# Pair attention on one core: the products of two steps made by one VectorE instruction for each half of the fields

## The reference

```
p = x[:, ROW, :]
q = x[:, COL, :]
inner = p * q
h = jax.nn.relu(jnp.einsum('bpe,he->bph', inner, W1) + b1)
logits = jnp.einsum('bph,oh->bpo', h, W2) + b2
attn = jax.nn.softmax(logits, axis=1)
pooled = jnp.sum(inner * attn, axis=1)
return pooled @ Wl.T + bl
```

## Time and profile before

| what | us |
|---|---|
| median of three runs | 1154.47 (1153.91 to 1154.53) |
| the profiled execution | 1153.29 |
| its span in the trace | 1151.4 |
| PE busy (matmuls) | 1128.6 (98%) |
| DVE busy | 1056.9 (92%) |
| ACT busy | 982.9 (85%) |

### The profile page before, as it was taken

The page is one execution under the profiler, slowest core; times in us unless marked ns, Lnnn a source line. Parts: engine busy times, 40 slices in busy tenths (PEclk is TensorE's granted clock), DMA queues, the critical chain, the costliest instruction groups (busy, mean ns, idle before and its releaser), DMA issues.

```text
span 1151.4 us, 63299 instructions
## 1 busy us (share of the span) xinstructions
PE 1128.6 (98%) x29001; PEld 534.3 (46%) x29001; DVE 1056.9 (92%) x1691; ACT 982.9 (85%) x1219; POOL 0.7 (0%) x6
## 2 busy tenths in 40 slices
PE   6999999999999999999999999999999999999995
PEld 3444444444444444444444444444444444444442
DVE  7999999899999989999899998999999999998983
ACT  5888888888888888888888888888888888888884
POOL 0000000000000000000000000000000000000000
PEclk9999999999999999999999999999999999999997
DMA  2221221222121121211312212121122213113010
GB/s 58 42 66 32 61 39 29 62 40 55 36 60 35 37 64 29 66 29 34 69 28 63 40 26 66 35 59 37 30 63 39 57 34 68 30 35 69 14 43 2
DMA packets 220376, 51.31 MB, mean 45 GB/s; under 512 B 216016, under 2 KB 216016, under 8 KB 220112
## 3 DMA queue, kind: packets, MB, share of 16 engines
q1 hardware_dynamic: 220112, 47.27, 20.0%
HBM read 34.11 MB, written 13.12 MB: 41 GB/s over the span
## 4 chain that ended last, share of the span: by engine, by line
PE 98%; DVE 1%; SPq 1%; ACT 0%; DMA 0%; issue 0%; ACTq 0%
PE slot L296 60%; PE logit_bank L316 29%; PE slot L277 4%; PE slot L264 4%; DMA x_rows<-in_r_x 0%; PE slot L342 0%; SPq L193 0%; ACT hidden L369 0%; DVE weighted L468 0%; SPq L223 0%; SPq L227 0%; SPq L225 0%; SPq L230 0%; DVE logits L448 0%; DVE row_max L452 0%
## 5 line engine op out<-in xcount | busy, mean ns | idle before, releaser
L369 ACT ACTIVATE hidden<-slot,b_col 128x780 f32<-128x780 f32 x1024 | 875.9, 909 | 115.9 <-PE slot L296 115.8
L431 DVE TENSOR_TENSOR inner<-xt 128x760 f32<-128x760 f32 x1024 | 909.5, 943 | 58.8 <-PE slot L296 58.1
L296 PE MATMUL slot<-inner,w_block 64*32 64x390 f32 x16384 | 782.8, 490 | 0.0
L296 PEld LDWEIGHTS slot<-inner,w_block 64*32 64x32 f32 x16384 | 300.7, 107 | 326.4 <-issue 281.5
L316 PE MATMUL logit_bank<-hidden,w_window 64*32 64x390 f32 x8192 | 442.1, 487 | 0.6 <-ACT hidden L369 0.6
L316 PEld LDWEIGHTS logit_bank<-hidden,w_window 64*32 64x32 f32 x8192 | 152.8, 105 | 186.4 <-ACT hidden L369 81.5
L277 PEld LDWEIGHTS slot<-xt,x_scaled 64*40 64x40 f32 x4096 | 45.4, 117 | 40.6 <-issue 40.6
L353 ACT COPY xt<-slot 128x640 f32<-128x640 f32 x64 | 44.4, 694 | 19.6 <-PE slot L264 19.6
L361 ACT COPY gram_rows<-slot 128x640 f32<-128x640 f32 x64 | 44.4, 694 | 18.3 <-PE slot L277 18.3
L438 DVE TENSOR_TENSOR inner<-xt 128x80 f32<-128x80 f32 x256 | 59.5, 233 | 0.0
L264 PE MATMUL slot<-ident,x_rows 128*128 128x128 f32 x320 | 50.1, 288 | 9.3 <-DMA x_rows<-in_r_x 9.3
(11 more groups left out here) (28 smaller groups left out, 27.2 us busy)
## 6 DMA issues: line engine op xcount, KB each, us to landing
x_rows<-in_r_x SPq DMA_DIRECT2D x128, 160.0 KB, 3.0
gram<-gram_dram SPq DMA_DIRECT2D x32, 400.0 KB, 3.7
gram_dram<-gram_rows SPq DMA_DIRECT2D x512, 12.5 KB
gram_dram<-gram_rows SPq DMA_DIRECT2D x256, 25.0 KB
w_rows<-in_L_rec_W SPq DMA_DIRECT2D x2, 16.0 KB, 2.3
wl_col<-in_L_rec_Wl SPq DMA_DIRECT2D x2, 0.2 KB, 2.3
b_col<-in_L_rec_b SPq DMA_DIRECT2D x2, 0.2 KB, 2.3
w_window<-in_L_rec_W SPq DMA_DIRECT2D x2, 0.2 KB, 2.3
```

The lines of the kernel that those rows point to most:

```text
L296: last = nc.tensor.matmul(banks[to:to + QUAD, ab * BANK:ab * BANK + HALF], w1_block[rows, of:of + QUAD], inner[rows, at:at + HALF], start= ...
L369: nc.scalar.activation(hidden[s % RING][:, half * PAIRS:(half + 1) * PAIRS].rearrange("p (a n) -> p a n", a=2), banks_of("layer", s, half) ...
L431: nc.vector.tensor_tensor(window_view(inner, to + half * HALF, [[PAIRS, STEP_DUOS], [SPAN, SHIFTS], [1, SPAN]]), window_view(fields, at + ...
```

## The change

`products` is called for even steps only and makes both steps of the pair. Each half is now one instruction of 4 duos x 380 products. The tail is put between the two halves, so that the first half of both steps is complete after two instructions. A pair of steps adds 3 to `inner_ready` in place of 5, and TensorE waits before each half: for 2 of the 3 before the first half, for all 3 before the second. The place in the ring that VectorE waits for before a pair is now that of the pair's second step, `s + 1 - 8`.

```diff
-        def inner_to(s):
-            return 5 * (s // 2 + 1)
+        def inner_to(s, half):
+            return 3 * (s // 2) + 2 + half
...
             def first_layer(s, half):
-                if half == 0:
-                    pe.wait_ge(inner_ready, inner_to(s))
+                pe.wait_ge(inner_ready, inner_to(s, half))
...
-                    act.wait_ge(inner_ready, inner_to((n - XT_RING + 1) * CHUNK_STEPS - 1))
+                    act.wait_ge(inner_ready, inner_to((n - XT_RING + 1) * CHUNK_STEPS - 1, 1))
...
             def products(s):
                 if s >= INNER_RING:
-                    dve.wait_ge(slots_filled, count_to("layer", s - INNER_RING, 1))
-                fields = xt[n % XT_RING]
+                    dve.wait_ge(slots_filled, count_to("layer", s + 1 - INNER_RING, 1))
+                fields, duos = xt[n % XT_RING], 2 * STEP_DUOS
                 for half in range(2):
                     nc.vector.tensor_tensor(
-                        window_view(inner, to + half * HALF, [[PAIRS, STEP_DUOS], [SPAN, SHIFTS], [1, SPAN]]),
-                        window_view(fields, at + half * SPAN, [[EXT, STEP_DUOS], [0, SHIFTS], [1, SPAN]]),
-                        window_view(fields, at + half * SPAN + 1, [[EXT, STEP_DUOS], [1, SHIFTS], [1, SPAN]]),
+                        window_view(inner, to + half * HALF, [[PAIRS, duos], [SPAN, SHIFTS], [1, SPAN]]),
+                        window_view(fields, at + half * SPAN, [[EXT, duos], [0, SHIFTS], [1, SPAN]]),
+                        window_view(fields, at + half * SPAN + 1, [[EXT, duos], [1, SHIFTS], [1, SPAN]]),
                         ALU.mult).then_inc(inner_ready, 1)
-                if s % 2:
-                    to, at, duos = to - STEP, at - STEP_DUOS * EXT, 2 * STEP_DUOS
-                    nc.vector.tensor_tensor(
+                    if half == 0:
+                        nc.vector.tensor_tensor(
+                            window_view(inner, to + SHIFTS * SPAN, [[PAIRS, duos], [HALF, 2], [1, LAST]]),
...
             for s in range(STEPS):
-                products(s)
+                if s % 2 == 0:
+                    products(s)
```

More of the change, by code:

```diff
@@ L431, in products @@
                     nc.vector.tensor_tensor(
-                        window_view(inner, to + half * HALF, [[PAIRS, STEP_DUOS], [SPAN, SHIFTS], [1, SPAN]]),
-                        window_view(fields, at + half * SPAN, [[EXT, STEP_DUOS], [0, SHIFTS], [1, SPAN]]),
-                        window_view(fields, at + half * SPAN + 1, [[EXT, STEP_DUOS], [1, SHIFTS], [1, SPAN]]),
+                        window_view(inner, to + half * HALF, [[PAIRS, duos], [SPAN, SHIFTS], [1, SPAN]]),
+                        window_view(fields, at + half * SPAN, [[EXT, duos], [0, SHIFTS], [1, SPAN]]),
+                        window_view(fields, at + half * SPAN + 1, [[EXT, duos], [1, SHIFTS], [1, SPAN]]),
                         ALU.mult).then_inc(inner_ready, 1)
-                if s % 2:
-                    to, at, duos = to - STEP, at - STEP_DUOS * EXT, 2 * STEP_DUOS
-                    nc.vector.tensor_tensor(
[L439 to L442, removed]
+                    if half == 0:
+                        nc.vector.tensor_tensor(
+                            window_view(inner, to + SHIFTS * SPAN, [[PAIRS, duos], [HALF, 2], [1, LAST]]),
+                            window_view(fields, at, [[EXT, duos], [SPAN + LAST, 2], [1, LAST]]),
+                            window_view(fields, at + SPAN, [[EXT, duos], [SPAN + LAST, 2], [1, LAST]]),
+                            ALU.mult).then_inc(inner_ready, 1)
             def softmax_of_round(r):
```

## The result

The changed kernel takes 1171.59 us (median of 6 runs, 1170.72 to 1174.78) against 1154.35 us (6 runs, 1153.91 to 1154.99). The ratio over all these runs is given as 1.0158, with a 95% interval of 1.0148 to 1.0169; the two medians alone give 1.0149. By the medians it is 17.2 us more, where 15.6 were forecast. The profiled execution has a span of 1168.9 us.

A forecast was written before the change was run, and what follows sets the result against it. TensorE was taken as the bound, with VectorE setting its time only at 15 hand-overs. The copy late by 1.04 us at each adds 15.6 us: 1154.47 + 15.6 = 1170.1, predicted as 1170, range 1164 to 1176 (8 in 10).

The forecast's parts named there:

- TensorE is the bound, and VectorE decides only at the hand-overs: TensorE's chain sets the time; only at 15 hand-overs between rounds does VectorE's copy hold a score, by 0.14 us.
- The longer products: On VectorE, each 1520-element instruction lasts 1.74 us; 0.14 us saved for each of 256 pairs, 35 us, hidden behind TensorE.
- The copy late by 1.04 us, 15 times: At each hand-over the copy of the scores starts at 508.67, not 507.63, delaying TensorE's score: 15.6 us in all.
- The first halves' signal: Before TensorE's first layers: products lie about 9 us ahead, so having them sooner gives TensorE's chain nothing.
- The extra wait costs nothing: Before each second half on TensorE: one more wait hides in 0.174 us of issue slack; otherwise, say, 5 us.
- The room that the range had for it: Some room above in the range, in case each of 512 extra TensorE waits took 0.01 us, 5 us.
- a score of 1.84 us: Sign in TensorE's chain at 15 hand-overs: the odd score lasts 0.66 + 0.14 + 1.04 = 1.84 us.
- VectorE as the bound: Rival, whole kernel: VectorE really sets the time, so its 35 us come off, giving 1119.5 us; chance 4%.
- The copy not late: Rival at the hand-overs: pairs start earlier or the relu is awaited, so time stays 1154 to 1156; chance 6%.
- The clock: Rival at the hand-overs: TensorE's pauses lower its clock, adding about 1.9 us each, 44 us in all, 1199; chance 3%.
- The rule for grouping VectorE's work: Skill rule for a saturated VectorE: larger operations save about 60 ns each; alone, 31 us gained over 512 instructions.

The follow-up runs named there:

- e6: Changed kernel with the copy of the scores after step 5 and TensorE waiting once a step for the whole pair: 1153.84 us, ratio 1.0001 to the kernel before.
- e5: Changed kernel with copy after step 5, one TensorE wait a step, and Gram matrices ahead of the waiting score at hand-overs: 1151.52 us, ratio 0.9979.
- e7: Kernel before with only the Gram matrices put ahead of the waiting score at the hand-overs: 1151.01 us, ratio 0.9978.
- e2: Changed kernel with a ring of 10 steps in place of 8: 1155.28 us, ratio 1.0016 to the kernel before.
- e9: Changed kernel with both pairs ahead of the copy (4/5 and 6/7 of each round) made by step as before: 1155.64 us against 1153.54, ratio 1.0021.
- e8: Changed kernel with only the pair right ahead of the copy (6/7 of each round) made by step as before: 1174.42 us (2 runs), ratio 1.0180.
- e10: Kernel before with the copy of the scores after step 8 in place of step 7: 1173.86 us against 1153.54, ratio 1.0174.
- e1: Changed kernel with the copy of the scores after step 5 in place of step 7: 1155.70 us against 1154.16, ratio 1.0015.
- e4: Changed kernel with TensorE waiting once a step, before the first half, for all 3 signals of the pair: 1170.24 us, ratio 1.0137 to the kernel before.
- e3: Kernel before with TensorE waiting for the products before each second half too, 512 more waits: 1156.27 us against 1154.16, ratio 1.0017.

## Why the prediction was right, point by point

- *TensorE is the bound, and VectorE decides only at the hand-overs.* Right. e6 takes VectorE's busy time down by 38.7 us (1056.9 to 1018.2) and is at 1.0001; e5 and e7 aren't told apart.
- *The longer products.* 1.74 us forecast, 1737 ns measured; 35 us less busy, 35.1 measured. The line through three sizes held.
- *The copy late by 1.04 us, 15 times.* Right in the place, the path and the size: 7.60 us from the release of pair 4/5 to the copy were forecast, 7.62 measured; 1.06 us a round by the spacing of the copies. e2 and e9 show that the ring's wait for a whole pair does it, e8 that undoing the wait of the last pair alone gives nothing back, e10 that a late copy costs this much without any long instruction, e1 that nothing else in the change costs as much.
- *The first halves' signal.* Worth nothing, as forecast (e4).
- *The extra wait costs nothing.* This step failed, in a small term. "The issue has 0.174 us to spare" is true of the steady stretch and says nothing of the few places where issue stops for longer. e3 shows 2.1 us more by the medians; e1 against e6 has 1.9 and the changed kernel against e4 1.4, both not side by side. With 15.9 that makes 17.3 to 18.0, where 17.2 were measured. Not all that lies beyond the 15.9 in a single trace need be this: the 0.5 us ahead of the first copy are 1.0 in e4, which hasn't got the waits (88.43 - 86.33 - 1.06). The room that the range had for it was right by its size and not by its reasoning, since the cost isn't spread evenly over 512 waits. How a few more instructions come to such pauses, and why at these places, stays open: the trace shows that they end by "issue" and where they fall, not what the queue lacked. In the changed kernel's profile one of 0.90 us lies at 305.3, in one of the two odd rounds.
- *What would show it.* I expected a score of 1.84 us in the chain. The chain instead leaves TensorE at this place and runs along VectorE for 8.7 us, and the score has 0.89. The lateness reads from the wait row (14.5 us in 15 times) and from the copy's start. At the foot of that leg the layer reads 1.56 us where 1.47 is usual; the timeline gives it the usual 1.54 with its end (507.36 to 508.90), so I take it for the way the chain counts where it changes engine.
- *The rivals.* VectorE as the bound: out by e6. The copy not late: out by the rows above. The clock: the granted clock of the whole run is 0.995 against 0.994, it is 1.00 in every stretch from 20 to 1130 us, and the scores after TensorE's pause of 1 us last 0.89, as the last one did before. The price of this rival was poorly founded: it took the 64 matmuls in 4.54 us of the start for a stretch at a lower clock, but the granted clock there, from 10 to 16 us, is 1.00, so no row ties that length to the clock. The rule for grouping VectorE's work (the Trainium skill, Perfetto Trace Analysis, "Optimizing Scalar/DVE Operations") is borne out in its saving, 35.1 us over 512 instructions, 0.069 us each, and so is its condition: with VectorE not saturated none of this reached the end.

## What to carry to other kernels

When two instructions become one, look at the waits ahead of them: the joined one starts only when both places are free. Follow the engine's program from there to the next thing that the bounding engine waits for, in this kernel a copy that stood two pairs behind with 0.3 us to spare. If the work must stay joined, move that copy ahead of it or lengthen the ring, and put independent work of the bounding engine in front of its wait.

## What the runs showed that I had not expected

A wait on TensorE for something long past isn't free. When an instruction has another wait already, it becomes an instruction of its own (63811 records against 63299), and 512 of them among some 58,000 cost about 2 us, in pauses at a few places, of which the longest is 0.5 us in one kernel (e2) and 1.3 in another (e3). The runs also seem to spread wider with them: 2.9 to 4.0 us from lowest to highest in e1, e2, e3 and e9 (9 to 11 runs each), 1.8 to 2.0 in e5, e6 and e7 (11 each). The kernel before has 2.3 in 26 runs on one chip and 2.9 in 27 on another.
